# Attention in a fused decoder kernel: the causal mask moves from TensorE to VectorE, the subtraction of the maximum to GpSimd, and the order of the work changes

## The reference

```python
q, k, v = split(x @ w_attn.T + b_attn)        # 16 heads of 16
s = (q @ k.T) / sqrt(16)                      # per batch and head, 128 x 128
s = where(causal, s, -inf)                    # causal mask
p = softmax(s, axis=-1)
x = layernorm(x + (p @ v) @ w_proj.T + b_proj)
```

## Time and profile before

| | us |
|---|---|
| median of 3 runs (822.9 to 824.99) | 822.99 |
| the profiled execution | 823.1 |
| its span (first to last instruction) | 821.3 |
| PE busy | 745.7 (91%) |
| VectorE busy | 642.5 (78%) |
| GpSimd busy | 482.3 (59%) |
| ScalarE busy | 397.8 (48%) |

### The profile page before, as it was taken

One profiled execution on the slowest core, in us unless ns is written; L12 is line 12 of the kernel. 1 busy time (PEld: TensorE's weight loads), 2 busy tenths in 40 slices (PEclk: granted clock), 3 DMA queues, 4 the chain that ended last, 5 costly groups with the idle time before them and its releaser, 6 DMA issues. The chain is left out here.

```text
span 821.3 us, 13489 instructions
## 1 busy us (share of the span) xinstructions
PE 745.7 (91%) x4390; PEld 510.2 (62%) x4414; DVE 642.5 (78%) x1291; ACT 397.8 (48%) x641; POOL 482.3 (59%) x721
## 2 busy tenths in 40 slices
PE   6999999998999599999869999989899669999895
PEld 5677777764444277777647777765444337777674
DVE  3667777757999777774849999978999779988874
ACT  1555555553304344443676778860100036777785
POOL 1112333447776344441256777799878379899993
PEclk9999999999999799999989999989999969999998
DMA  7900000001100500000030221103000000000001
GB/s 272 363 2 2 1 2 2 1 2 73 80 1 0 196 1 1 1 2 1 0 132 37 67 70 61 51 2 119 1 0 0 1 0 1 1 20 14 14 21 39
DMA packets 12868, 33.97 MB, mean 41 GB/s; under 512 B 2688, under 2 KB 8064, under 8 KB 11520
## 3 DMA queue, kind: packets, MB, share of 16 engines
q1 hardware_dynamic: 12800, 33.11, 11.2%
HBM read 30.94 MB, written 2.16 MB: 40 GB/s over the span
## 5 line engine op out<-in xcount | busy, mean ns | idle before, releaser
L1081 PE MATMUL bank<-XT,win_late 128*128 128x256 f32 x320 | 87.9, 402 | 4.5 <-DVE ss_xc L1331 4.3
L467 POOL TENSOR_TENSOR at_kbd<-at_qk,at_hmask 128x512 f32<-128x512 f32 x16 | 16.6, 1040 | 113.5 <-DVE at_qk L394 113.5
L639 DVE TENSOR_REDUCE MIX<-m_pr 128x128 f32<-128x1024 f32 x64 | 77.3, 1211 | 0.4
L587 POOL TENSOR_TENSOR m_kv<-XT,CTXT 128x512 f32<-128x512 f32 x64 | 67.5, 1076 | 9.7 <-PE bank L612 9.7
L587 POOL TENSOR_TENSOR m_kv<-CTXT 128x512 f32<-128x512 f32 x64 | 65.0, 1038 | 12.2 <-PE bank L612 12.2
L1331 DVE SCALAR_TENSOR_TENSOR ss_xc<-bank,cw_late,ss_xc 128x254 f32<-128x254 f32 x144 | 66.5, 476 | 4.0 <-ACT ss_xc L1204 0.5
L1081 PEld LDWEIGHTS bank<-XT,win_late 128*128 128x128 f32 x320 | 56.9, 195 | 19.6 <-DVE ss_xc L1331 12.5
L610 PE MATMUL bank<-m_kv,toep 128*128 128x512 f32 x128 | 65.9, 596 | 2.8 <-POOL m_kv L587 2.8
L612 PE MATMUL bank<-m_kv,toep 128*128 128x512 f32 x128 | 65.4, 592 | 0.0
L611 PE MATMUL bank<-m_kv,toep 128*128 128x512 f32 x128 | 65.4, 592 | 0.0
L1634 PE MATMUL bank<-had_last,f_ht 128*128 128x256 f32 x256 | 61.8, 386 | 0.0
(11 more groups left out here) (233 smaller groups left out, 1893.8 us busy)
## 6 DMA issues: line engine op xcount, KB each, us to landing
MIX<-cum_rows SPq DMA_DIRECT2D x16, 512.0 KB, 3.7
toep<-toep_dram SPq DMA_DIRECT2D x2, 2048.0 KB, 11.5
X<-x_dram SPq DMA_DIRECT2D x1, 2048.0 KB, 12.2
CTXT<-ctxT_dram SPq DMA_DIRECT2D x1, 2048.0 KB, 17.6
out_dram<-f_o SPq DMA_DIRECT2D x16, 128.0 KB, 1.7
XT<-xT_dram SPq DMA_DIRECT2D x1, 1280.0 KB, 7.9
win_late<-win_dram SPq DMA_DIRECT2D x1, 1280.0 KB, 5.2
wgu<-wgu_dram SPq DMA_DIRECT2D x1, 1024.0 KB, 5.2
```

The lines of the kernel that those rows point to most:

```text
L587: m = nc.gpsimd.tensor_tensor(KV[n % 3][:, c, :, :].rearrange("p (b j) i -> p b j i", b=HB), ki, vj, ALU.mult)
L639: nc.vector.tensor_reduce(head(MIX)[:, :, a, bass.ts(h, HB), :], PR[n % 2][:, :, :, :].rearrange("p c (b j) i -> p c b j i", b=HB), op=ALU ...
L1081: m = nc.tensor.matmul(bX[(NU * g + n) % 3][:, 0:GS_], win[:, h, off:off + P], XT[:, h, bass.ts(g, GS_)], start=(h == 0), stop=(h == C - 1))
```

## The change

The mask tile in bfloat16, the eight mask matmuls per batch and the casts go. VectorE's new `mask` adds the mask (float32, one head wide, broadcast over four heads) while it moves the scores from PSUM to PR. `peak` then reads PR in SBUF instead of PSUM. `shift` becomes a GpSimd instruction that subtracts in place in PR. PR gets a third buffer, laid over two of the three `kv` buffers of the first mixer, so the mixer's step 1 on GpSimd waits until batch 14 has used its probabilities. The orders on all engines are new and the pipeline is deeper (`na = B + 11`): on TensorE `value`, `project`, `context_turn` and most `turn_p` come one step later, two of the four `times_v` one step later, `x_turn` three. On VectorE `residual` comes one step later. On GpSimd the residual's sum and `rstd` come one step earlier. The mixer still starts at step 18, and its first product now waits for the last `mask` instead of the last `shift`.

```diff
+    causal = ch.sb("at_causal", [P, S])
+    PR.append(T["m0_kv"][:, 1:3].rearrange("p k c b i -> p (k c b i)").rearrange("p (h s) -> p h s", h=H0))
...
     def score(n):
             pe.wait_ge(s["k_spread"], n + 1)
-            upto(pe, s["shifted"], 4 * n)
+            upto(pe, s["masked"], 4 * n)
             for g in range(2):
                 for t in range(4):
-                    nc.tensor.matmul(bS[t][:, bass.ts(g, 2 * S)], identb[:, :], mask[:, :, :], start=True, stop=False)
-                for t in range(4):
                     rows = slice(RT * t, RT * t + RT)
-                    m = nc.tensor.matmul(bS[t][...], QK[n % 3][rows, g, :], KBD[n % 2][rows, g, :, :], start=False, stop=True)
+                    m = nc.tensor.matmul(bS[t][...], QK[n % 3][rows, g, :], KBD[n % 2][rows, g, :, :], start=True, stop=True)
...
     TensorE, step(i)
             qk(i, 0)
+            times_v(i - 4, 2)
+            qk(i, 1)
+            times_v(i - 4, 3)
+            score(i - 1)
+            turn_p(i - 3, 0)
+            x_turn(i - 11)
+            turn_p(i - 3, 3)
+            value(i - 2)
+            project(i - 6)
+            context_turn(i - 5)
+            turn_p(i - 2, 1)
             times_v(i - 3, 0)
-            qk(i, 1)
+            turn_p(i - 3, 2)
             times_v(i - 3, 1)
             context_back(i - 4)
-            x_turn(i - 8)
-            times_v(i - 3, 2)
-            score(i - 1)
-            project(i - 5)
-            times_v(i - 3, 3)
-            turn_p(i - 2, 1)
-            context_turn(i - 4)
-            turn_p(i - 2, 0)
-            value(i - 1)
-            turn_p(i - 2, 3)
-            turn_p(i - 2, 2)
...
     ScalarE, step(i)
-            keep_p(i - 1, 1)
+            soften(i, 0)
+            keep_p(i - 1, 0)
+            keep_x(i - 9)
+            keep_p(i - 1, 3)
+            keep_v(i)
             keep_cn(i - 3)
-            keep_p(i - 1, 0)
-            keep_v(i)
-            keep_p(i - 1, 3)
+            keep_p(i, 1)
             keep_p(i - 1, 2)
             soften(i, 1)
-            keep_x(i - 6)
-            soften(i, 0)
             keep_ct(i - 1)
...
     VectorE
+        def mask(n, t):
+            dve.wait_ge(s["scored"], 4 * n + t + 1)
+            upto(dve, pt_made[t], n - 2)
+            nc.vector.tensor_tensor(PR[n % 3][:, 4 * t:4 * t + 4, :], bS[t][:, :].rearrange("p (h s) -> p h s", h=4),
+                                    causal[:, :].unsqueeze(1).broadcast_to([P, 4, S]), ALU.add).then_inc(s["masked"], 1)
         def peak(n, t):
-            dve.wait_ge(s["scored"], 4 * n + t + 1)
-            nc.vector.tensor_reduce(MX[n % 2][:, 4 * t:4 * t + 4], bS[t][:, :].rearrange("p (h s) -> p h s", h=4), ...
+            dve.wait_ge(s["masked"], 4 * n + t + 1)
+            upto(dve, s["shifted"], 4 * (n - 2) + t + 1)
+            nc.vector.tensor_reduce(MX[n % 2][:, 4 * t:4 * t + 4], PR[n % 3][:, 4 * t:4 * t + 4, :], ...
...
             keep_qk(i)
+            peak(i - 2, 2)
+            peak(i - 2, 3)
+            mask(i - 1, 0)
+            mask(i - 1, 1)
+            peak(i - 1, 0)
+            mask(i - 1, 2)
+            peak(i - 1, 1)
+            residual(i - 6)
+            mask(i - 1, 3)
             stats(i - 6)
             sums(i - 4)
             aggregate(i - 6)
             context(i - 4)
             norm_x(i - 7)
-            peak(i - 1, 1)
-            residual(i - 5)
-            peak(i - 1, 0)
-            peak(i - 1, 3)
-            peak(i - 1, 2)
-            shift(i - 1, 3)
-            shift(i - 1, 2)
-            shift(i - 1, 0)
-            shift(i - 1, 1)
...
     GpSimd
+        def shift(n, t):
+            pool.wait_ge(s["max_made"], 4 * n + t + 1)
+            v = PR[n % 3][:, 4 * t:4 * t + 4, :]
+            nc.gpsimd.tensor_tensor(v, v, MX[n % 2][:, 4 * t:4 * t + 4].unsqueeze(2).broadcast_to([P, 4, S]), ALU.subtract).then_inc(s["shifted"], 1)
...
             spread(i)
-            residual(i - 5)
-            rstd(i - 7)
+            shift(i - 1, 0)
+            shift(i - 1, 1)
+            residual(i - 4)
+            rstd(i - 6)
+            shift(i - 1, 2)
+            shift(i - 1, 3)
...
     mixer, GpSimd
+            if skip and n == 1:
+                pool.wait_ge(before["ct_made"], B - 1)
     mixer, TensorE
             if skip and n == 0:
-                pe.wait_ge(before["shifted"], 4 * B)
+                pe.wait_ge(before["masked"], 4 * B)
```

More of the change, by code:

```diff
@@ L168, in qk @@
                 upto(pe, s["qk_kept"], n)
-                upto(pe, pt_kept[0], n - 2)
-                upto(pe, s["proj_kept"], n - 5)
+                upto(pe, pt_kept[0], n - 3)
+                upto(pe, s["proj_kept"], n - 6)
             for g in (2 * h, 2 * h + 1):
@@ L190, in score @@
                 return
-            if n == 0:
-                pe.wait_ge(s["consts"], 2)
             pe.wait_ge(s["k_spread"], n + 1)
-            upto(pe, s["shifted"], 4 * n)
+            upto(pe, s["masked"], 4 * n)
             for g in range(2):
                 for t in range(4):
-                    nc.tensor.matmul(bS[t][:, bass.ts(g, 2 * S)], identb[:, :], mask[:, :, :], start=True, stop=False)
-                for t in range(4):
                     rows = slice(RT * t, RT * t + RT)
-                    m = nc.tensor.matmul(bS[t][:, bass.ts(g, 2 * S)], QK[n % 3][rows, g, :], KBD[n % 2][rows, g, :, :], start=False, stop=True)
+                    m = nc.tensor.matmul(bS[t][:, bass.ts(g, 2 * S)], QK[n % 3][rows, g, :], KBD[n % 2][rows, g, :, :], start=True, stop=True)
                     if g:
@@ L206, in turn_p @@
                 return
-            pe.wait_ge(s["exped"], 2 * n + 2 - t // 2)
+            pe.wait_ge(s["exped"], 2 * n + 1 + t // 2)
+            upto(pe, pt_kept[t], n)
             if t == 0:
-                upto(pe, pt_kept[0], n)
-                upto(pe, s["proj_kept"], n - 2)
-                upto(pe, s["qk_kept"], min(n + 3, B))
+                upto(pe, s["proj_kept"], n - 3)
+                upto(pe, s["qk_kept"], min(n + 4, B))
             elif t == 2:
-                upto(pe, pt_kept[2], n)
                 upto(pe, s["cn_kept"], n - 1)
-                upto(pe, s["x_kept"], n - 5)
+                upto(pe, s["x_kept"], n - 7)
             elif t == 1:
@@ L219, in turn_p @@
                 upto(pe, pt_kept[3], n)
+                upto(pe, s["back_kept"], n - 2)
+            else:
                 upto(pe, s["back_kept"], n - 1)
-            else:
                 pe.wait_ge(pt_kept[1], n + 1)
             for r in range(4):
-                m = nc.tensor.transpose(bPT[t][:, bass.ts(r, S)], PR[n % 2][:, 4 * t + r, :], ident[:, :])
+                m = nc.tensor.transpose(bPT[t][:, bass.ts(r, S)], PR[n % 3][:, 4 * t + r, :], ident[:, :])
             m.then_inc(pt_made[t], 1)
@@ L245, in context_back @@
             pe.wait_ge(pt_kept[3], min(n + 2, B))
+            pe.wait_ge(pt_kept[1], min(n + 3, B))
             for j in range(4):
@@ L255, in context_turn @@
             upto(pe, s["cn_kept"], n)
-            upto(pe, s["x_kept"], n - 3)
+            upto(pe, s["x_kept"], n - 5)
             for h in range(C):
@@ L264, in project @@
             pe.wait_ge(s["cn_kept"], n + 1)
-            pe.wait_ge(pt_kept[0], min(n + 3, B))
-            pe.wait_ge(s["qk_kept"], min(n + 6, B))
+            pe.wait_ge(pt_kept[0], min(n + 4, B))
+            pe.wait_ge(s["qk_kept"], min(n + 7, B))
             upto(pe, s["proj_kept"], n)
@@ L275, in x_turn @@
             pe.wait_ge(s["ln_done"], n + 1)
-            pe.wait_ge(pt_kept[2], min(n + 6, B))
-            pe.wait_ge(s["cn_kept"], min(n + 4, B))
+            pe.wait_ge(pt_kept[2], min(n + 8, B))
+            pe.wait_ge(s["cn_kept"], min(n + 6, B))
             upto(pe, s["x_kept"], n)
@@ L309, in scalar @@
         nc.scalar.copy(identb[:, :], ident[:, :])
-        nc.scalar.copy(mask[:, :, :], maskf[:, :, :]).then_inc(s["consts"], 1)
+        act.wait_ge(s["consts"], 1)
         def keep_p(n, t):
@@ L321, in soften @@
                 return
-            act.wait_ge(s["shifted"], 4 * n + 4 - 2 * half)
-            v = PR[n % 2][:, 8 * half:8 * half + 8, :]
+            act.wait_ge(s["shifted"], 4 * n + 2 + 2 * half)
+            v = PR[n % 3][:, 8 * half:8 * half + 8, :]
             nc.scalar.activation(v, v, ACT.Exp, scale=HD0 ** -0.5).then_inc(s["exped"], 1)
@@ L370, in vector @@
         dve.wait_ge(s["proj_in"], 48)
+        def mask(n, t):
+            if not 0 <= n < B:
+                return
+            if n == 0:
+                dve.wait_ge(s["value_in"], 48)
+            dve.wait_ge(s["scored"], 4 * n + t + 1)
+            upto(dve, pt_made[t], n - 2)
+            nc.vector.tensor_tensor(PR[n % 3][:, 4 * t:4 * t + 4, :], bS[t][:, :].rearrange("p (h s) -> p h s", h=4),
+                                    causal[:, :].unsqueeze(1).broadcast_to([P, 4, S]), ALU.add).then_inc(s["masked"], 1)
         def peak(n, t):
@@ L374, in peak @@
                 return
```

(13 more changed lines are left out.)

4 lines of the change are left out of this document (1 added, 3 removed).

## The result

| | before | after |
|---|---|---|
| median, us (17 runs each) | 822.99 (820.87 to 825.91) | 826.56 (824.46 to 829.43) |
| profiled execution, us | 823.1 | 826.81 |
| its span | 821.3 | 825.0 |

The ratio is 1.0043, with a 95% interval of 1.0029 to 1.0056: slower by 0.3 to 0.6%. The forecast was 819.2 us, faster by 0.5%. The measured time lies within the wide range (811 to 829), outside the sum's own range (815 to 824), and on the other side of no change.

What follows compares the result with a forecast made beforehand. TensorE bounds attention and the mixer's steady part, a ring the handover between. Of 18.4 us (masks) and 4.3 (moved work), 3.9 remains at product 9: 823.1 - 3.9 = 819.2 us; own range 815 to 824, wide range 811 to 829.

Steps and rivals of the forecast that it cites:

- What bounds the kernel: TensorE carries attention at 10.6 us a step and the mixer's steady part; a ring of engines paces the handover.
- Mask products: Attention on TensorE: dropping eight a batch saves 1.15 us, between 1.08 and 1.30; 18.4 us over 16 batches.
- VectorE and GpSimd: Attention step: VectorE stays about 7.7 us, GpSimd rises to 8.1, both fitting a new step of 9.45.
- The waits of the new order: Full attention steps: added latency stays covered, VectorE 0.9 us to spare, GpSimd 1.4; priced at nothing.
- (b): Rival, nine full attention steps: the loop score, addition, maximum, shift sets 10.8 us a step; 832 us; chance 0.11.
- Step 18: Attention's step 18 on TensorE begins at 152.5 instead of 175.20: 18.4 us from masks, 4.3 from moved work.
- Product 0: Mixer's first product starts 8.5 us after step 18, at 161.0 instead of 178.63: 17.6 earlier.
- The handover: From step 18 to mixer product 9: most gain goes; product 3 comes 4.1 us earlier, product 9 3.9 earlier.
- The ring: Handover, n = 1 to 3: product, multiplication, residual, stats, aggregate, rstd, kv, next product; 9.3 us a trip; chance 0.70.
- The later end: Everything after the mixer is unchanged, so product 9's shift, 3.9 us earlier, is the whole time's shift.
- (a): Rival at the handover: the ring is not closed and TensorE carries the gain through; about 805 us; chance 0.07.
- (c): Rival: thin spares lose 0.2 to 0.4 us a step; 821 to 823, no change to be seen; chance 0.12.

Runs made afterwards that it cites:

- e5: e1's kernel with the eight mask products a batch put back on TensorE, VectorE still adding its mask: 822.1 us, ratio 0.9999 to before.
- e2: Changed kernel, ring kept, TensorE doing identity products before waiting for kv in the mixer's first four products: 818.97 us, ratio 0.9938 to before.
- e1: Changed kernel with GpSimd's residual sum and rstd one step later from step 18 on, opening the ring: 802.59 us, ratio 0.9753 to before.
- e4: Changed kernel with only rstd one step later on GpSimd from step 18 on, residual left in place: 807.69 us, ratio 0.9813 to before.
- e6: e1's kernel with the mixer's kv also one step earlier on GpSimd: 800.21 us, ratio 0.972 to before.
- e3: Kernel before the change with only GpSimd's rstd one step earlier from step 18 on, closing the ring: 841.55 us, ratio 1.0224 to before.

## Why the prediction was wrong, point by point

**What bounds the kernel: right.** TensorE carried attention; taking products off it shortened the step at once.

**Mask products: right.** 1.15 was taken from 1.08 to 1.30. The step fell by 1.3 with the score alone (2.37 to 1.08), the high end, and e5 puts the whole at 1.2 a batch (19.5 us, where the sum had 18.4).

**VectorE and GpSimd: right, with one size off.** The subtraction is 1043 ns (1.04 forecast), the addition 680 (683). The maximum from SBUF is 674, not 605: halving the mixer's reduction was wrong, the 0.68 end was right. It cost nothing, VectorE being covered. Beside the shifts the additions took 678 to 683 ns and the maxima 673 to 677 in every case of 60 to 130 us, so they were never held up, as the prediction expected.

**The waits of the new order: right.** No engine made TensorE wait in the full steps; rival (b) is out. norm_x had a median of 404 ns and at most 762 between 60 and 130 us.

**Step 18: right, forecast 2.6 us too late.** 149.88 instead of 152.5; the step was 9.28, not 9.45. With the mask products back (e5) step 18 starts at 169.42, 5.8 before that of the kernel before, where the sum had 4.3 for moved work: 1.5 of the 2.6 us lie there, and where exactly is not shown; the rest is the mask term.

**Product 0: right.** 158.76 instead of 161.0: 8.9 behind step 18, not 8.5.

**The handover: mechanism right, one term missing; this is the step that failed.** The ring closed for n = 1, 2 and 3 as forecast. But the prediction says "9.3 us for one step" and takes each product at its duration at the full clock. It even forecast "TensorE idle half that time", and did not ask what such idleness does to the granted clock. The loss to the clock stood in the sum at nothing, without a reason; it measured 8.7 us, and the trips were 11.3, 11.2 and 10.9. In numbers: product 9 was forecast at 205.9. Product 0 came 2.2 us earlier than the sum, the three trips without the clock's part were 0.5 shorter (27.4 for 27.9), and the way from product 3 to product 9 was 0.3 shorter; the lower clock cost 8.7: 205.9 - 3.0 + 8.7 = 211.6, and 211.70 was measured. With the clock kept (e2), the trips are 8.9 to 9.4. None of the signs that the prediction named for being wrong (steps over 9.9, products 5 us apart) covers trips near 11. In the kernel before, the idle stretches in the handover were 2.3 us at most at a clock of 1.00, so it had no row at the lower level there, and the trip that I read from it was one at the full clock. But its trace has such rows right behind the mixer, where TensorE stands idle for 4.71 us up to 274.17. TensorE in the order of time, and the window over the first group, before:

```profile
280.50 3.19 PE L723 MATMUL bank<-wgu,f_qt 128*128 128x512 bf16 x7 [0.44 <-ACT f_qt L795]
...
286.41 1.52 PE L723 MATMUL bank<-wgu,f_qt 128*128 128x512 bf16 x6
```

```profile
280.50:283.40 2.90, 2.90 (x7) 1.03 (x7) 1.26 (x6) 1.53 (x2) 2.43 (x8) 0.50 0.99 417
```

The same records follow each other at 0.43 us there (seven in 2.99, up to the next group at 283.49) and at 0.23 six microseconds later (six in 1.36, up to 287.77), where the clock is 1.00 again. (The DMA engines were busy beside the slow ones, 0.99 of the window; the granted clock of 0.50 alone accounts for the factor.) These rows could have priced the term. The section of the Trainium skill named above gives the idle state half the full clock, and I did not weigh it.

**The later end.** Product 9 was taken as the measure of the whole. Over five variants it is that within 2.7 us: product 9 came 22.7, 5.2, 14.1 and 25.3 us earlier in e1, e2, e4 and e6 and 17.3 later in e3, and the medians moved by 20.9, 4.5, 15.8, 22.6 and 18.1. For the change it is 1.9 of 3.6 us; in e5 product 9 came 2.8 us earlier and the median 0.7. The rest of the program, from the first sum of the feed-forward stage to the span's end, took 546.4 us before and 548.5 after, but 546.3 to 549.4 over the six experiments, with no order in it. Whether the remaining 1.7 us is such scatter or belongs to the change was not settled.

**Rivals.** (a) was out as a forecast, but it is what the kernel does once the ring is open: 802.6 against its 805. (b) and (c) did not happen. The prediction gave "slower" 0.12, for (b)'s loop; that it came out slower was another mechanism, and that the time still lies in the wide range is luck.

## What to carry to other kernels

Where two pipelines are interleaved, look for a ring through the in-order queues at the seam: if engine A's step i waits for something in engine B's same step, and B's step stands behind A's result of the step before, the seam runs at the sum of the latencies. Three short instructions (rstd's two and the residual's sum, 1.5 us of GpSimd) placed one step earlier cost 24 us here and hid a gain of 20. Whenever a sum leaves TensorE idle for microseconds, price its next products at the lower clock as well, and look through the whole trace, other stages too, for a row after such a gap.

## What the runs showed of the hardware that was not expected

- Products of 2.57 us took 4.1 to 5.3 us after idle stretches of 3.4 to 5.5 us (granted clock 0.50 to 0.64); after a stretch of 1.6 us in e1 the clock stayed at 1.00. Filling them with small products brought 7.6 us back.
- The clock need not have fallen while TensorE was idle. In e4 it was still 1.00 in the idle stretch ahead of product 1 (163.5 to 166.8); the first two records of the product took 1.22 us, little more than the usual 1.02 to 1.12, the next two 1.91, and the granted clock from 167.87 to 171.20 was 0.51.
- A maximum over 128x512 costs VectorE 674 ns from SBUF and 682 from PSUM: moving the source saves nothing. Over 1024 elements it is 1209.
- norm_x (VectorE, out of and into SBUF) can be held up by GpSimd: it took 404 ns at the median of the full steps, but up to 1.12 us in e4, where it had begun 0.07 us after GpSimd's kv (two instructions of 1.04 us):

```profile
164.71 2.08 POOL L601 TENSOR_TENSOR m_kv<-CTXT 128x512 f32<-128x512 f32 x2
164.78 1.12 DVE L527 TENSOR_SCALAR X<-at_y,at_mv,at_rs 128x256 f32<-128x256 f32 x1 [0.48 <-POOL at_rs L521]
```
